# An early-fusion transformer block on one core: attention in six rounds of four score blocks in place of eight rounds of three, with the second round's VectorE work in another order

## What is computed

```python
h = tok(x, W_embed, b_embed, pos_embed)
h = jnp.concatenate([h, txt], axis=1)
h = h + attn(layernorm(h), Wq, Wk, Wv, Wo, bo)      # 16 heads of 16, causal, softmax
h = h + ffn(layernorm(h), w_up, w_down)             # ternary weights, RMS norm before each, GELU
```

## Time and profile before

| what | value |
|---|---|
| median of 3 runs | 2010.46 us (2006.98 to 2012.05) |
| profiled execution | 2009.03 us |
| its span, first to last instruction | 2007.3 us |
| TensorE busy | 1924.2 us, 96% |
| VectorE busy | 1469.4 us, 73% |
| ScalarE busy | 1312.9 us, 65% |
| GpSimd busy | 890.5 us, 44% |
| granted TensorE clock | 0.981 of full |

### The profile page before, as it was taken

One profiled execution on the slowest core, in us unless ns is written; L12 is line 12 of the kernel. 1 busy time (PEld: TensorE's weight loads), 2 busy tenths in 40 slices (PEclk: granted clock), 3 DMA queues, 4 the chain that ended last, 5 costly groups with the idle time before them and its releaser, 6 DMA issues.

```text
span 2007.3 us, 59820 instructions
## 1 busy us (share of the span) xinstructions
PE 1924.2 (96%) x25090; PEld 1571.7 (78%) x25090; DVE 1469.4 (73%) x2720; ACT 1312.9 (65%) x1986; POOL 890.5 (44%) x1064
## 2 busy tenths in 40 slices
PE   5789999999999999999999999999999999999975
PEld 4668888888888888888888888888888888888754
DVE  4667777877777777777787777777777778777754
ACT  4346776676767667677667676666667766667652
POOL 1124444554444454444455444445444445444442
PEclk8889999999999999999999999999999999999988
DMA  5011111101111111111110111111111121010000
GB/s 152 20 38 45 52 50 56 51 29 52 42 55 51 52 44 36 46 51 51 55 51 28 52 42 55 51 53 40 38 45 52 51 55 51 29 52 17 30 29 24
DMA packets 66116, 93.72 MB, mean 47 GB/s; under 512 B 10082, under 2 KB 59718, under 8 KB 65592
## 3 DMA queue, kind: packets, MB, share of 16 engines
q1 hardware_dynamic: 65848, 89.90, 15.8%
HBM read 45.03 MB, written 14.94 MB: 30 GB/s over the span
## 4 chain that ended last, share of the span: by engine, by line
PE 89%; ACT 3%; DVE 3%; issue 2%; POOL 1%; DMA 1%; SPq 0%; DVEq 0%; POOLq 0%; ACTq 0%
PE dense L324 50%; PE score L324 21%; PE pvps L324 9%; PE dense L342 3%; PE dense L381 3%; ACT qm L702 2%; PE dense L555 2%; PE dense L370 1%; POOL acc L1184 1%; DMA h<-txt 1%; DVE mx L956 1%; ACT pr L677 0%; DMA pix<-x 0%; DVE st L940 0%; DVE mx L955 0%
## 5 line engine op out<-in xcount | busy, mean ns | idle before, releaser
L1165 POOL TENSOR_SCALAR_AFFINE_SELECT pr<-pr 114x456 f32<-114x456 f32 x512 | 311.5, 632 | 851.0 <-ACT pr L677 851.0
L677 ACT ACTIVATE pr<-score 114x1368 f32<-114x1368 f32 x256 | 335.7, 1311 | 300.3 <-PE score L324 300.0
L955 DVE TENSOR_REDUCE mx<-score 114x4 f32<-114x456 f32 x256 | 161.3, 630 | 257.4 <-PE score L324 255.7
L956 DVE TENSOR_REDUCE mx<-score 114x4 f32<-114x912 f32 x256 | 281.4, 1099 | 0.0
L324 PE MATMUL dense<-wdn,g 128*114 128x256 bf16 x1024 | 242.5, 282 | 2.6 <-DVE gl L927 1.4
L324 PE MATMUL score<-qm,km 32*114 32x228 f32 (+1 forms) x4096 | 220.8, 330 | 18.7 <-DVE mx L956 15.4
L324 PE MATMUL dense<-wdn,gl 128*114 128x256 bf16 x1024 | 235.5, 275 | 0.0
L1184 POOL TENSOR_TENSOR acc<-acc,sq 128x456 f32<-128x456 f32 x192 | 222.6, 1159 | 18.9 <-POOL acc L1184 0.4
L324 PEld LDWEIGHTS score<-qm,km 32*114 32x114 f32 x4096 | 175.2, 174 | 69.3 <-issue 40.5
L324 PE MATMUL score<-km,qm 32*114 32x114 f32 (+1 forms) x4096 | 221.7, 331 | 7.4 <-ACT pr L677 6.7
L324 PE MATMUL pvps<-pr,vp 114*32 114x228 f32 (+1 forms) x4096 | 204.9, 317 | 1.0 <-ACT raw L744 0.6
(11 more groups left out here) (125 smaller groups left out, 4401.7 us busy)
## 6 DMA issues: line engine op xcount, KB each, us to landing
pix<-x SPq DMA_DIRECT2D x64, 588.0 KB
rs<-raw SPq DMA_DIRECT2D x256, 57.0 KB, 2.0
cx<-raw SPq DMA_DIRECT2D x256, 57.0 KB, 2.0
out<-h SPq DMA_DIRECT2D x64, 228.0 KB
h<-txt SPq DMA_DIRECT2D x32, 64.0 KB, 7.2
km<-wqkvo SPq DMA_DIRECT2D x1, 1024.0 KB, 13.6
h<-w_upT SPq DMA_DIRECT2D x1, 1024.0 KB, 14.0
km<-w_embed SPq DMA_DIRECT2D x1, 768.0 KB, 6.9
```

What stands on the lines that cost most here:

```text
L677: act(pr[q % 2][:], score[0:R, :, 0:SW], ACT.Exp, scale=float(HD) ** -0.5).then_inc(a["exp"], 1)
L955: nc.vector.tensor_reduce(mx[:, m, 0, x:128:32], score[0:R, :, 0:R], AX.X, ALU.max)
L956: nc.vector.tensor_reduce(mx[:, m, 1, x:128:32], score[0:R, :, R:SW], AX.X, ALU.max).then_inc(v["max"], 1)
L1165: nc.gpsimd.affine_select(out=blocks, in_=blocks, compare_op=ALU.is_ge, fill=0.0, base=0, pattern=[[0, 4], [1, R]], channel_multiplier=-1) ...
```

## The change

The score banks now hold four blocks of 114 columns in place of three, and a step has six rounds in place of eight. The tables `ROWS`, `COLUMNS` and `VALUES` say for each third of a sequence which head group r, which block and which slot of the bank. The same blocks are computed as before: eight groups of three blocks are six groups of four. A mask matmul covers three or two blocks, and there are 16 of them in each of six rounds in place of eight. `exponential` reads and writes four blocks, `maxima_unit` reduces two times 912 elements, and `causal` is one instruction over three or two blocks in place of two over one. The values stand in front of the column scores in a round and use the round before's `pr`.

All else that stood in eight rounds is spread over six. `gelu_lo`, of which GpSimd had three in eight, is VectorE's alone. The second half of the pixels is loaded into `sq`, and `reorder` of it runs at the start of the step that uses it. `cx` and `raw` lie in one tensor. In round k = 1 VectorE takes the low parts of two pixel groups, the maxima, `scale_of`, and then the low part of the third pixel group; ScalarE takes `normalized` in front of the exponential.

```diff
-SW = S + R
+ROUNDS = 6
...
+ROWS = [[(0, 1, 0), (1, 0, 2), (0, 0, 3)], [(1, 1, 0), (2, 1, 2)], [(3, 1, 0), (3, 0, 2), (2, 0, 3)]]
+COLUMNS = [[(0, 0, 2), (0, 1, 1), (1, 1, 0)], [(1, 0, 0), (2, 0, 2)], [(3, 0, 2), (3, 1, 1), (2, 1, 0)]]
+
+VALUES = [[(0, 0, 0, 2), (0, 1, 0, 1)], [(1, 0, 0, 0), (1, 1, 1, 0)],
+          [(2, 0, 1, 2), (2, 1, 0, 0), (3, 0, 0, 2), (3, 1, 0, 1)]]
...
+        def values_of(t, k):
+
+            return (t - 2, k + 1) if k < 5 else (t - 1, 0)
 
         def score_emptied(t, k, columns):
 
...
-                for kb in range(2):
+                for r, kb, slot in COLUMNS[third]:
+                    m, par = divmod(r, 2)
                     c0 = b * S + kb * R
                     for i in range(4):
-                        last = mm(score[0:R, i, kb * S:S + kb * R], km[quad(i), buf, m, par, c0:c0 + R],
+                        last = mm(score[0:R, i, slot * R:(slot + 2 - kb) * R], km[quad(i), buf, m, par, c0:c0 + R],
                                   qm[quad(i), par, buf, m, c0:b * S + S], start=True, stop=True,
                                   skip_group_check=True)
                 last.then_inc(pe["st"], 1)
 
...
-                for qb in range(2):
+                for r, qb, slot in ROWS[third]:
+                    m, par = divmod(r, 2)
...
+                every = 2 if third == 1 else 1
+                n = 4 - every
...
-                P_ = pr[gi % 2]
-                half = r % 2
-                for kb in range(2):
+                for r, kb, back, slot in VALUES[third]:
+                    half = r % 2
                     for i in range(4):
                         last = mm(pvps[quad(i), half * S + kb * R:half * S + S],
                                   vp[:, par + 1 if b else 0, kb, 8 * (r // 2) + 2 * i + half],
-                                  P_[:, i, kb * S:S + kb * R], start=(kb == 0), stop=(kb == 1),
+                                  pr[(q - back) % 2][:, i, slot * R:(slot + 2 - kb) * R], start=(kb == 0), stop=(kb == 1),
                                   skip_group_check=True)
...
                     if Bm:
...
                     if A and k == 1:
                         pixels(t, 3)
                         pixels(t, 4)
+                        embed(t, 0, 0)
                         pixels(t, 5)
-                    if A and k == 2:
-                        embed(t, 0, 1)
                     if Dd and k == 2:
-                        eng.wait_ge(a["xn2"], count(4, t - 3, 4))
...
+                    if A and k == 5:
                         queries_keys(t, 0)
+                    weighted_values(t, u, k)
                     scores_columns(t, u, k)
-                    if A and k == 7:
-                        queries_keys(t, 2)
-                    pair, gi = (t - 2, k + 2) if k < 6 else (t - 1, k - 6)
-                    if live(pair):
-                        weighted_values(pair, u if k < 6 else 1 - u, gi)
+                    if Bm and k == 0:
+                        values(t - 1, 0)
                     if A and k == 0:
                         pixels(t, 0)
                         pixels(t, 1)
                         pixels(t, 2)
...
-                        embed(t, 0, 0)
...
+                        embed(t, 0, 1)
+                    if Dd and k == 1:
+                        eng.wait_ge(a["xn2"], count(4, t - 3, 4))
+                        to_columns(t - 3, "x2t", 0, xn)
+                        to_columns(t - 3, "x2t", 1, xn)
+                    if Bm and k == 2:
+                        maxima_rows(t - 1, 0)
+                    if A and k == 2:
                         embed(t, 1, 0)
                         embed(t, 1, 1)
...
-                if q >= 2:
-                    eng.wait_ge(pe["pv"], count(8, pair, q - 1))
+                if q >= 1:
+                    eng.wait_ge(pe["pv"], count(ROUNDS, pair, q))
                 elif began(pair - 1):
-                    eng.wait_ge(pe["pv"], count(8, pair - 1, 7 + q))
-                eng.wait_ge(pe["st"], count(8, pair, q + 1))
-                act(pr[q % 2][:], score[0:R, :, 0:SW], ACT.Exp,
+                    eng.wait_ge(pe["pv"], count(ROUNDS, pair - 1, ROUNDS))
+                eng.wait_ge(pe["st"], count(ROUNDS, pair, q + 1))
+                act(pr[q % 2][:], score[0:R, :, 0:4 * R], ACT.Exp,
...
+                eng.wait_ge(pe["pv"], count(ROUNDS, pair, (2, 3, 5, 6)[k]))
...
+                    if A and t > 0 and k == 0:
+                        reorder(t, 1)
                     if A and k == 1:
                         pixels_hi(t, 3)
                         pixels_hi(t, 4)
                         pixels_hi(t, 5)
...
-                    exponential(t, k)
-                    if A and k == 0:
-                        pixels_hi(t, 0)
-                        pixels_hi(t, 1)
-                        pixels_hi(t, 2)
                     if Dd and k == 1:
                         if began(t - 4):
                             eng.wait_ge(pe["x2t"], count(2, t - 4, 2))
                         eng.wait_ge(pe["xt"], count(2, t - 1, 2))
...
+                    if Cc and k in (0, 1, 3, 4):
+                        unscaled(t - 2, k if k < 2 else k - 1)
+                    if A and k == 5:
+                        if began(t - 1):
+                            eng.wait_ge(pe["v"], count(2, t - 1, 2))
+                        hi_part("xt", 0, aT[0], t)
+                        hi_part("xt", 1, aT[0], t)
+                        queries(t, u, 0)
+                        odd_keys(t, u, 0)
+                    exponential(t, k)
+                    if Bm and k == 0:
+                        value_rows(t - 1, 1 - u, 0)
+                    if A and k == 0:
+                        pixels_hi(t, 0)
+                        pixels_hi(t, 1)
+                        pixels_hi(t, 2)
+                    if A and k == 1:
+                        hidden_columns(t, 0)
...
+                    if Dd and k == 1:
+                        if began(t - 4):
+                            eng.wait_ge(pe["up"], count(8, t - 4, 8))
+                        hi_part("x2t", 0, xT2[0], t - 3)
+                        hi_part("x2t", 1, xT2[0], t - 3)
...
-                    if following and k in (6, 7):
-                        reorder(t + 1, k - 6)
+                    if following and k == 5:
+                        reorder(t + 1, 0)
...
+                    if A and k == 1:
+                        pixels_lo(t, 3)
+                        pixels_lo(t, 4)
...
+                    if Bm:
+                        maxima_unit(t - 1, k)
...
-                    if A and k == 1:
-                        pixels_lo(t, 3)
-                        pixels_lo(t, 4)
-                        pixels_lo(t, 5)
                     if Dd and k == 1:
                         scale_of(t - 3)
+                    if A and k == 1:
+                        pixels_lo(t, 5)
                     if Cc and k == 1:
                         collect(t - 2, 0)
...
-                    if A and k == 4:
+                        for m in range(8):
+                            gelu_lo(t - 3, m)
+                    if Cc and k == 2:
+                        collect(t - 2, 1)
+                    if Bm and k == 2:
...
                     eng.wait_ge(pe["mt"], count(2, pair, 1))
-                x = 16 * (1 - par)
-                nc.vector.tensor_reduce(mx[:, m, 0, x:128:32], score[0:R, :, 0:R], AX.X, ALU.max)
-                nc.vector.tensor_reduce(mx[:, m, 1, x:128:32], score[0:R, :, R:SW], AX.X,
-                                        ALU.max).then_inc(v["max"], 1)
+                if third == 1:
+                    nc.vector.tensor_reduce(mx[:, 0, 1, 0:128:32], score[0:R, :, 0:2 * R], AX.X, ALU.max)
+                    nc.vector.tensor_reduce(mx[:, 1, 1, 16:128:32], score[0:R, :, 2 * R:4 * R], AX.X,
+                                            ALU.max).then_inc(v["max"], 1)
+                else:
+                    m, x = third // 2, 16 - 8 * third
+                    nc.vector.tensor_reduce(mx[:, m, 1, x:128:32], score[0:R, :, 0:2 * R], AX.X, ALU.max)
+                    nc.vector.tensor_reduce(mx[:, m, 0].rearrange("p (i y d) -> p i y d", i=4, y=2)[:, :, :, 0],
+                                            score[0:R, :, 2 * R:4 * R].rearrange("p i (y w) -> p i y w", y=2), AX.X,
+                                            ALU.max).then_inc(v["max"], 1)
...
-                for c0 in (0, S):
-                    blocks = pr[gi % 2][:, :, c0:c0 + R]
-                    nc.gpsimd.affine_select(out=blocks, in_=blocks, compare_op=ALU.is_ge, fill=0.0, base=0,
-                                            pattern=[[0, 4], [1, R]], channel_multiplier=-1).then_inc(p["mask"], 1)
-
...
+                first, every, n = (0, 2, 2) if gi % 3 == 1 else (0, 1, 3)
+                blocks = pr[gi % 2][:].rearrange("p i (x w) -> p i x w", w=R)[:, :, first:3:every]
```

(35 more changed lines are left out.)

352 lines of the change are left out of this document (145 added, 207 removed), and 6 rows, old and new, of the table DENSE.

## The result

The changed kernel takes **2026.3 us** (median; 2024.7 to 2028.1) against 2010.8 us of the kernel before on the same chip: a ratio of **1.0083, interval 1.0068 to 1.0097**. The medians are 15.5 us apart; by the ratio it is 17. The forecast was 2023, in a range of 2001 to 2045. The profiled execution spans 2025.7 us, 18.4 more than the one before.

The account below looks back on a forecast made before the run. TensorE's work was taken as the bound, plus waits opened in the step: -1.2 + 1.7 + 0.2, +0.75 us a step, +22 over 29 steps, -8 filling, end equal; +14 on 2009 gives 2023 us, range 2001 to 2045.

Parts of the forecast that it names:

- The sign and the mechanism: Slower, 2023 us: in round k = 1 the later normalization delays the exponential, whose bank TensorE's next row scores need.
- Every station of the chain: Second round, counted from its row scores' start X: maxima X + 3.54, scale 5.56, normalized 6.64, exponential 9.08, next row scores 10.85.
- TensorE's own work: Per step, fewer and wider pieces in six rounds save TensorE 1.2 us, bounds 0.3 and 1.5.
- The first two rivals: Second-round chain hidden, 1969 us, chance 12%; mask's matmul time by number of matmuls alone, 2008 us, chance 10%.
- The wait of the second round: In round k = 1 TensorE waits 1.7 us a step for the exponential before the next row scores.
- a gap anywhere else: Stated sign of being wrong: TensorE idle elsewhere than between the x2t transposes and round 2's row scores.
- The third rival: A further wait in rounds 0, 2 or 4; one margin failing by 1 us gives 2050 us; chance 12%.
- The wait of `up` 0: After round 2's row scores, `up` 0 waits for the bank of the x2t transposes, 0.2 us more a step.
- the term of +22 us: The 29 steady steps each go from 59.26 to 60.0 us, +0.75 us a step, +22 us together.
- The filling steps: The two filling steps at the start take 8 us less, bounds 2 and 11.
- The end: The last three steps come out equal: two fewer hand-overs against rounds a quarter longer and the same second-round chain.
- Edits at no cost: Gelu low parts on VectorE, single-instruction selects, half-by-half pixel loads cost nothing; a failed cover loses 1 to 2 us a step.

Follow-up runs that it names:

- run 1: The change with VectorE taking the second normalization's scale first in round k = 1, ahead of pixel parts and maxima; 1999.3 us, ratio 0.9953.
- run 4: The change with one more ScalarE operation of 256 elements (0.50 us) ahead of the four normalized of the second normalization; 2040.6 us, ratio 1.017.
- run 3: The change with ScalarE doing unscaled and the exponential ahead of the four normalized in the second round; 2084.1 us, ratio 1.039.
- run 5: The change with VectorE's second round ordered scale, one pixel part, maxima, then the other two pixel parts; 1985.1 us, ratio 0.987.
- run 11: The change with only GpSimd's causal select of the first round moved ahead of its power; 2026.0 us, ratio 1.010.
- run 12: run 5 with GpSimd's select ahead of its power, and maxima ahead of the scale in steps without pixels; 1988.6 us, ratio 0.990.
- run 9: run 5 with GpSimd's select ahead of its power, and column scores ahead of the values in the last two steps; 1985.6 us, ratio 0.988.
- run 10: The kernel before with all eight low parts of the gelu on VectorE in their round, none on GpSimd; 2040.2 us, ratio 1.016.
- run 2: The change with the scale ahead of the maxima on VectorE, behind the two pixel parts; 2007.4 us, ratio 1.0001.

## Why the prediction was right, and where only the total was

**The sign and the mechanism** were right. That a later normalization holds the exponential, and this the next row scores, is shown by run 1 (start it earlier: both waits go), run 4 (lengthen it: slope 0.48 for 0.50) and run 3 (it isn't ScalarE's order: the other order waits for the normalization itself). Every station of the chain was within 0.1 us. The Trainium skill (Perfetto Trace Analysis, Optimizing Scalar/DVE Operations) says that smaller operations may finish sooner where an engine that isn't saturated opens bubbles on another. The sign of this case agrees, but no run here tests the size by itself, and the same sizes gave 2026 and 1985 us by order alone (run 5).

**TensorE's own work** was foreseen at -1.2 us a step. Without idle time the step went from 59.11 (59.26 - 0.15) to 57.83 us (1677.09 / 29), -1.28. The pieces, from start to start: rows 0.86 to 0.88, mask 0.45 and 0.35, columns 0.98, values 0.72 and 1.30, against 0.87, 0.47 and 0.35, 0.98, 0.72 and 1.29. The first two rivals are out: nothing was hidden, and the mask's matmul of 342 columns takes 307 ns, 51 more than 228 columns do, 0.45 ns a column.

**The wait of the second round** was foreseen at 1.7 us. In run 5 the round up to the next row scores takes 9.44 us, 9.14 without its wait of 0.30; in the change it takes 10.80: 1.66 us. It comes as three waits (0.31, 0.15, 1.10), and the rest I put down to lost overlap, which no run isolates. The forecast saw it in one place and took a gap anywhere else as a sign of being wrong; the two small gaps are such places, though the long one ends where it said. The third rival's wait in rounds 0, 2 or 4 did not come in the steady steps: the view of waits has these three there and no other.

**The wait of `up` 0**, 0.2 us, did not come: 0.00 us idle there. This, 0.1 us of further saving and roundings make the step 59.58 in place of 60.0; the term of +22 us measured +9.1.

**The filling steps**, -8 us, were the weakest estimate: -2.0 in one pair of profiles, -5.3 in the other. In the first pair the step in front of them took back 1.0.

**The end** was the step that failed: "the last three steps come out equal". They are 10.3 us longer: 5.5 of idle time (40.9 against 35.4) and 4.8 of busy time (106.2 against 101.4), at a granted clock of 0.80 against 0.85. Taken between the powers, the three parts of the end are 5.2, 3.1 and 1.3 us longer, and 0.7 lies in front of the first of these powers. The third rival's mechanism, the power in front of the select, was at work there and not in the steady steps:

```profile
1942.30 1.64 POOL L1195 TENSOR_TENSOR pw<-ve,exps 114x8 f32<-114x8 f32 x1 [5.25 <-DVE ve L1092]
1943.90 1.42 POOL L1174 TENSOR_SCALAR_AFFINE_SELECT pr<-pr 114x1368 f32<-114x1368 f32 x1
1943.97 1.35 DVE L1010 TENSOR_TENSOR rm<-pw 114x4 f32<-114x4 f32 x1 [1.75 <-POOL pw L1195]
...
1945.37 2.51 PE L340 MATMUL pvps<-pr,vp 114*32 114x228 f32 x32 [4.41 <-POOL pr L1174]
```

But it does not set the end: removing it (run 11) gave 0.2 us, the order of run 12 nothing, and that of run 9 cost 4.2. In a step without dense work to fill in, each round is a bare chain of exponential, select and values, and taking one wait away showed the next. Which part of the 10.3 us belongs to the longer pieces and which to the order stays open.

So the total, +14 foreseen and +18.4 measured, hit through errors that cancelled: 13 us too much in the steps, 7 too little at the start, 10 too little at the end. That the total came so close is luck.

**Edits at no cost** held in this arrangement (TensorE's wait for `gl` is 1.4 us in the whole run), but the reason given, that nobody waits for `gl`, is not what decides: in run 10 nobody does either, and it costs 30 us through what stands behind it.

## What to carry to other kernels

When an engine gets a new order, walk the chain of what it releases, station by station, from rows of the old trace: that was good to 0.1 us here. Put short work that starts another engine's long work (the scale, 1 us for five small instructions) ahead of long work that is waited for later (the maxima, 2 us); that alone turned a loss of 0.8% into a gain of 0.5% (run 1), and with one pixel part moved behind the maxima as well, into one of 1.3% (run 5). The first and last steps of a software pipeline are a kernel of their own: walk them separately. And an edit is free only if nothing behind it in its queue is waited for. Measure a stretch between marks that the edit itself doesn't move.

## What the runs showed of the hardware

GpSimd and VectorE exclude each other in some pairs of operations. A VectorE multiply of 4 elements a row, all operands in SBUF, took 0.95 us beside GpSimd's select and ended with it, and 0.15 to 0.17 us with GpSimd done. In runs 1 and 5 each, 31 of the 32 multiplies of the profile ran beside a select, and all 62 ended 0.01 to 0.02 us behind it. Near the end of the changed kernel it took 1.35 us (the row at 1943.97 above), again up to the select's end; the pixels' low parts, with one operand in PSUM, ran at full speed beside GpSimd's power (1.51 us for three, as in the earlier trace rows). The Trainium skill, SBUF — State Buffer, "SBUF: two separate sides", says that the two engines share a port pair under an exclusive lock, which a VectorE operation with two SBUF inputs needs against a GpSimd operation that reads SBUF. The traces agree in both cases, with 0.8 us lost for one tiny instruction.

TensorE's clock fell after waits of 1.79 us in three of four steps of run 3 (0.61 over the next 3.5 us) and of 2.00 us at the end of the changed kernel. It did not after the same 1.79 us in every fourth step of run 3, nor after the waits of 1.2 us in run 2 and of 1.10 us in the steady steps of the change. So the length of the wait alone did not decide it. At the end of the changed kernel:

```profile
1879.34:1889.95 10.61, 8.24 (x137) 7.33 (x131) 8.75 (x19) 3.24 (x4) 3.03 (x2) 0.98 0.07 24
1889.95:1898.72 8.77, 8.52 (x104) 6.68 (x105) 3.97 (x10) 6.37 (x9) 1.42 (x1) 0.50 0.09 29
```

There 8.8 us of nearly unbroken work ran at 1.2 GHz behind it. In run 3 a wait of 1.79 us cost another 1.6 us by the clock, so a wait's price can be nearly twice its length.
